# State-space weights taken in the transposed layout, first maxima without transposes between them, gathers that start before the weights are in

## The reference

```
h = emb[x]                                       # 2 x 2048 tokens, 256 wide
Q, K, V = heads(h @ w + b)                       # 16 heads of 16
o = softmax(Q K^T / 4) V ; h = o @ wo + bo
xn = layernorm(h)
for each direction (forward; backward on the flipped sequence):
    xh, z = split(xn @ in_w.T)                   # in_w 1024 x 256
    xc = silu(causal 4-tap convolution of xh)
    dt, Bm, Cm = split(xc @ xproj_w.T)           # xproj_w 48 x 512
    delta = softplus(dt @ dt_w.T + dt_b)         # dt_w 512 x 16
    state-space scan over the sequence; y = (scan + xc * D) * silu(z)
    add y @ out_w.T to h                         # out_w 256 x 512
h = h + low_rank_ffn(layernorm(h))
```

## Time and profile before

| | us |
|---|---|
| median of 3 runs | 3738.87 |
| lowest and highest | 3728.02, 3742.55 |
| the profiled execution's own time | 3733.11 |
| its span in the profile | 3731.3 |
| its mean granted TensorE clock | 0.946 |

### The profile page before, as it was taken

How to read it: one execution, slowest core, us unless ns; L and a number is a source line. 1 busy time by engine, 2 the same in 40 slices (tenths; PEclk the granted TensorE clock), 3 DMA queues, 4 the chain that set the end, 5 groups by cost and what they waited for, 6 DMA issues and landing times. The chain is left out here.

```text
span 3731.3 us, 70349 instructions
## 1 busy us (share of the span) xinstructions
PE 3335.9 (89%) x24001; PEld 1935.0 (52%) x24001; DVE 2932.7 (79%) x3002; ACT 2798.2 (75%) x4818; POOL 1536.1 (41%) x1252
## 2 busy tenths in 40 slices
PE   7699999999999999745999999999999999987798
PEld 4333333333333333232666767667766767665554
DVE  2579999899989999241899889988899899998122
ACT  2158888788878888713988888988889888986133
POOL 3000000000000000001888888888888898888000
PEclk9669999899989999977999999999999999999899
DMA  5530202022020200042111111211111111111422
GB/s 171 134 74 6 39 5 39 12 33 34 10 39 5 40 5 5 19 165 59 41 58 47 57 58 58 68 60 56 56 48 58 57 58 58 52 52 62 138 73 79
DMA packets 102538, 203.95 MB, mean 55 GB/s; under 512 B 19328, under 2 KB 36768, under 8 KB 100704
## 3 DMA queue, kind: packets, MB, share of 16 engines
q1 hardware_dynamic: 81616, 174.28, 16.5%
q10 hardware_dynamic: 19088, 21.37, 2.0%
q0 software_dynamic: 1536, 4.20, 0.5%
HBM read 144.23 MB, written 55.05 MB: 53 GB/s over the span
## 5 line engine op out<-in xcount | busy, mean ns | idle before, releaser
L1071 POOL TENSOR_TENSOR m_g<-m_hs,m_cb 128x512 f32<-128x512 f32 x1024 | 1296.3, 1290 | 215.5 <-DVE m_hs L1369 205.0
L657 DVE TENSOR_REDUCE a_mx<-a_ps_m 128x2 f32<-128x1024 f32 x1024 | 1244.2, 1224 | 122.0 <-PE a_ps_m L505 100.2
L627 ACT ACTIVATE a_probs<-a_ps_s 128x512 f32<-128x512 f32 x2048 | 1111.6, 596 | 201.8 <-PE a_ps_s L535 144.6
L1369 DVE TENSOR_TENSOR_SCAN m_hs<-m_da,m_carry,m_ps_x 128x512 f32<-128x512 f32 x768 | 956.8, 1270 | 104.5 <-PE m_ps_x L1144 64.0
L505 PE MATMUL a_ps_m<-a_k,a_q 48*128 48x512 f32 x2048 | 790.9, 469 | 31.7 <-DMA a_q<-q_scr 28.4
L535 PE MATMUL a_ps_s<-a_q,a_k 50*128 50x512 f32 x2048 | 773.5, 457 | 20.8 <-issue 10.7
L1144 PE MATMUL m_ps_x<-m_ident,m_bu 128*128 128x128 f32 x4096 | 637.8, 279 | 107.4 <-DVE m_hs L1369 95.3
L1287 ACT ACTIVATE m_da<-m_delta,m_a_cur 128x512 f32<-128x512 f32 x1024 | 720.7, 713 | 5.7 <-DVE m_hs L1369 5.6
L1144 PEld LDWEIGHTS m_ps_x<-m_ident,m_bu 128*128 128x128 f32 x4096 | 484.5, 143 | 448.9 <-issue 324.6
L542 PE MATMUL a_ps_o<-a_probs,a_v 128*32 128x256 f32 x8192 | 665.1, 397 | 8.7 <-ACT a_o L614 8.2
L1272 ACT ACTIVATE m_bu<-m_dut,m_bt 128x512 f32<-128x512 f32 x896 | 639.3, 714 | 27.3 <-PE m_ps_x L1144 27.1
(11 more groups left out here) (158 smaller groups left out, 2325.8 us busy)
## 6 DMA issues: line engine op xcount, KB each, us to landing
m_cb<-c_scr SPq DMA_DIRECT2D x128, 512.0 KB, 3.8
y_scr<-m_ysb SPq DMA_DIRECT2D x16, 1024.0 KB, 6.7
ffn_y<-y_scr SPq DMA_DIRECT2D x16, 1024.0 KB, 10.2
a_k<-k_scr SPq DMA_DIRECT2D x96, 128.0 KB, 7.5
a_q<-q_scr SPq DMA_DIRECT2D x96, 128.0 KB, 9.8
q_scr<-p_partsq SPq DMA_DIRECT2D x16, 512.0 KB, 3.3
k_scr<-p_partsk SPq DMA_DIRECT2D x16, 512.0 KB, 3.3
m_xn<-xn_scr SPq DMA_DIRECT2D x16, 512.0 KB, 4.9
```

Of the source, the lines that this page charges most:

```text
L627: nc.scalar.activation(probs[:, t % PR, HEADS[j]], turned(i), ACT.Exp, scale=float(DK) ** -0.5).then_inc(exped, 1)
L657: nc.vector.reduce_max(mx[:, i:i + wide], ps_m[:, b:b + wide], AX.X).then_inc(m_maxed, 1)
L1071: nc.gpsimd.tensor_tensor(g[:, t % NG], hs[:, t % NHS], cb[:, quarter % 2, n % CQ], ALU.mult).then_inc(g_ok, 1)
L1369: nc.vector.tensor_tensor_scan(hs[:, t % NHS, rev], da[:, t % NDA, rev], ps_x[:, t % NX, rev], carry[:, n, i:i + 1] if p else 0.0, ALU.mul ...
```

## The change

The four state-space weights of each direction are handed to the program already in the layout in which it uses them (`laid_out`, on the host, before the launch). `weight_transposes` and its scratch tensors are gone: eight loads, 64 transposes, their copies and eight stores. The later stages load the same bytes in the same shapes from the inputs. Of the four memsets of ones, the two for the second buffer go from DVE to POOL. In the embedding stage `rows_free` is raised before PE's waits for `ids_ok` and `w_in`; POOL still waits for `ids_ok` by itself.

```diff
@@ embed_and_project, PE
                 nc.tensor.transpose(ps_t[:, 0, 0:NI], ids_f[:, 3], ident[0:NI, 0:NI]).then_inc(ids_col, 1)
+                pe.sem_inc(rows_free, 2)
                 pe.wait_ge(ids_ok, ONE + 1)
                 pe.wait_ge(w_in, ONE + 96)
-                pe.sem_inc(rows_free, 2)
...
@@ attention
-        W_AFTER = BLK + HG * EARLY - w_count
-        W_NEG = w_count - HG * (EARLY - 2)
+        FIRST_NEG = BLK + 8
...
@@ attention, SyncE
                 load(0, 0, [0, 1], first_parts)
-                sp.wait_ge(ones_ok, ONE + 2)
+                sp.wait_ge(ones_first, ONE + 2)
                 load(0, 0, [0, 1], last_part)
                 load(0, 0, range(2, HG))
                 store_neg(0, 0, 0)
-                sp.wait_ge(ones_ok, ONE + 4)
+                sp.wait_ge(ones_ok, ONE + 2)
                 load(1, 1)
...
@@ attention, GpSimd
                 identity(nc.gpsimd, ident32[:, :], a_cleared, ident32_ok)
-                w_clear()
+                pool.wait_ge(ident32_ok, ONE + 1)
+                for i, first in enumerate((P // 4, 3 * P // 4)):
+                    nc.gpsimd.memset(k_st[first:first + P // 4, 1].bitcast(FP32), 1.0).then_inc(ones_ok, 1)
+                    pool.wait_ge(ones_ok, ONE + i + 1)
...
@@ attention, PE
-                max_blocks(0, 0, 0, 0, W_AFTER, loads)
-                for i in range(w_count):
-                    w_transpose(pe, i)
-                    if i == W_NEG:
+                for item in range(BLK + HG * EARLY):
+                    if item == FIRST_NEG:
                         transpose_neg(0)
-                    item = W_AFTER + i
                     max_blocks(item // BLK, 0, item // BLK, item % BLK, item % BLK + 1, loads if item < BLK else None)
-                pe.wait_ge(w_copied, ONE + w_count)
...
@@ attention, ACT
-                w_load(act)
-                for i in range(w_count):
-                    if i == W_NEG:
-                        copy_neg(0)
-                    w_copy(act, i)
-                w_store(act)
+                copy_neg(0)
...
-                act.wait_ge(w_stored, ONE + 8 * 16)
...
@@ attention, DVE
-                for buf in range(2):
-                    for first in (P // 4, 3 * P // 4):
-                        nc.vector.memset(k_st[first:first + P // 4, buf].bitcast(FP32), 1.0).then_inc(ones_ok, 1)
+                for first in (P // 4, 3 * P // 4):
+                    nc.vector.memset(k_st[first:first + P // 4, 0].bitcast(FP32), 1.0).then_inc(ones_first, 1)
...
@@ mamba, SyncE (and the like for xproj_w, dt_w and, in mamba_out_and_ffn, out_w)
-                    sp.dma_start(win[:, :, 0:DI], win_scr[z][:, 0:DI].rearrange("(k p) m -> p k m", p=P)).then_inc(win_x, 16)
+                    sp.dma_start(win[:, :, 0:DI], win_t[z][:, 0:DI].rearrange("(k p) m -> p k m", p=P)).then_inc(win_x, 16)
```

More of the change, by code:

```diff
@@ L305, in attention @@
-def attention(nc, sem, q_scr, k_scr, v_all, o_scr, weights):
+def attention(nc, sem, q_scr, k_scr, v_all, o_scr):
     with ExitStack() as ctx:
@@ L1018, in _ @@
                     sp.dma_start(a_cur[:, z], w["A_log"].rearrange("(k p) n -> p k n", p=P)).then_inc(w_in, 16)
[L1019 removed]
+                    sp.dma_start(wxp[:, z], xp_t[z]).then_inc(w_in, 16)
                     for first in (X_DT, X_DT2):
[L1021 removed]
+                        sp.dma_start(wdt[first:first + R, z], dtw_t[z]).then_inc(w_in, 16)
                 load_xn(1)
@@ L1383, in _, with mamba_out_and_ffn @@
                     gate(STEPS - 1, i)
-def mamba_out_and_ffn(nc, sem, y_scr, ow_scr, h_scr, u1, v1, b1, u2, v2, b2, out):
+def mamba_out_and_ffn(nc, sem, y_scr, ow_t, h_scr, u1, v1, b1, u2, v2, b2, out):
     NF = FF // P
@@ L1621, in lm_tower @@
     dirs = [{n: a[f"L0_attn_{z}_{n}"] for n in names} for z in "fb"]
+    win_t, xp_t, dtw_t, ow_t = ([w[n] for w in dirs] for n in ("in_w", "xproj_w", "dt_w", "out_w"))
     with nc.sbuf_tensor("v_all", [P, B, H // HG, NT, HG * DK], FP32) as v_all:
@@ L1627, in lm_tower @@
         with semaphores(nc) as sem:
-            attention(nc, sem, q_scr, k_scr, v_all, o_scr, (dirs, win_scr, xp_scr, dtw_scr, ow_scr))
+            attention(nc, sem, q_scr, k_scr, v_all, o_scr)
     with semaphores(nc) as sem:
@@ L1631, in lm_tower, with laid_out @@
     with semaphores(nc) as sem:
-        mamba(nc, sem, dirs, win_scr, xp_scr, dtw_scr, xn_scr, y_scr, c_scr)
+        mamba(nc, sem, dirs, win_t, xp_t, dtw_t, xn_scr, y_scr, c_scr)
     with semaphores(nc) as sem:
-        mamba_out_and_ffn(nc, sem, y_scr, ow_scr, h_scr, a["L0_ffn_U1"], a["L0_ffn_V1"], a["L0_ffn_b1"],
+        mamba_out_and_ffn(nc, sem, y_scr, ow_t, h_scr, a["L0_ffn_U1"], a["L0_ffn_V1"], a["L0_ffn_b1"],
                           a["L0_ffn_U2"], a["L0_ffn_V2"], a["L0_ffn_b2"],
                           out.rearrange("b (t p) d -> (b t) p d", p=P))
+def laid_out(name, value):
+    if name.endswith("_in_w") or name.endswith("_dt_w"):
+        return value.T
+    if name.endswith("_xproj_w"):
+        rows = np.zeros((XPW, DI), value.dtype)
+        for first, part in ((X_DT, slice(0, R)), (X_DT2, slice(0, R)), (X_B, slice(R, R + DS)), (X_C, slice(R + DS, R + 2 * DS))):
+            rows[first:first + part.stop - part.start] = value[part]
+        return rows.T.reshape(ND, P, XPW).transpose(1, 0, 2)
+    if name.endswith("_out_w"):
+        return value.T.reshape(ND, P, D).transpose(1, 0, 2)
+    return value
 def kernel(**inputs):
```

74 lines of the change are left out of this document (5 added, 69 removed).

## The result

| | before | after |
|---|---|---|
| median, us | 3733.44 (4 runs) | 3677.81 (4 runs) |
| lowest and highest, us | 3727.89, 3742.55 | 3664.22, 3690.49 |
| ratio, 95% interval | | 0.986 [0.983, 0.989] |
| the profiled execution's span, us | 3731.3 | 3662.4 |

The change is faster by 55.6 us in this comparison. So a fair figure for the gain is about 44 us, give or take 5, and the profiled execution after, the fastest of the 14, is not a typical one. What made it faster than the others is told with the jumps.

A forecast was written before the change was run, and what follows sets the result against it. Two early stretches were taken as on the path, 125 to 228 us held by PE's transposes at half clock. Terms 2.9 + 8.4 + 30.2 + 4.2 = 45.7 us off gave 3687.4 or 3693.2 by baseline; forecast 3690, range 3676 to 3704.

The forecast's parts named there:

- Gathers: Embedding stage: index copy no longer waits behind PE's weight wait, so PE's transposes start earlier; -2.9 us, between -1.5 and -3.1.
- First loads: Attention start: without weight loads on ACT's queue, first keys and queries land at 141.8, not 150.2; -8.4 us, -3 to -8.9.
- The later load that served as the measure: The same 24 DMAs alone, from 406.44 us: twelve are in 14.4 us after the first issue.
- First maxima: Maximum scores before the body: 42 pairs at 1.14 us without transposes, 47.8 instead of 78.0; -30.2 us, or -25.6 at 1.25.
- ACT: Body's start: no weight stores ahead of ACT's first exponential, so it follows the first score sooner; -4.2 us, -3.5 to -4.4.
- The clock: PE's half clock in the early body, 0.42 us lost per microsecond; left at 0, ends -5.3 and +6.
- The rest was to shift by 46 us: Sign of being right: everything after the first exponential shifted by 46 us, the body's 32 reduces in 40 us unchanged.
- Half clock far beyond the body's first 26 us: Sign of being wrong: half clock in the attention body lasting far beyond its first 26 us or so.
- Early clock: Rival: the clock rises during the first maxima, so the body starts at 2.4 GHz; 5.3 us more gained, 3685; chance 0.15.
- Small terms: Rival: loads at most 3 us earlier, reduces at 1.25, gathers worth 1.5; 11.4 us less gain, 3701; chance 0.19.
- Low clock in the body: Rival: half clock stays in the body; 109 us beyond the 12.6 eats the gain; slower, chance 0.02.
- Nothing in the maxima: Rival: something other than the transposes holds the first stretch; 3.9 + 4.2 + 8.4 = 16.5 us gained, near 3720; chance 0.03.

The follow-up runs named there:

- repeats: The changed kernel's own runs plus two experiments that turned out to be it over again; 14 runs, median 3686.4 us (3664.22 to 3697.06).
- stores_kept: Changed kernel with ACT's eight stores of the earlier sizes put back, writing the values' buffer to scratch nobody reads; 3686.59 us, ratio 0.989.
- after_sem127: Changed kernel with 127 increments of an unused semaphore in PE's list at the attention stage's start; 3699.43 us, ratio 0.991.
- transposes_kept: Changed kernel with 64 transposes of a constant put back between the maximum scores, and ACT's 64 copies, without loads or stores; 3721.84 us, ratio 0.997.

## Why the prediction was right

The forecast was 3690.0, and the changed kernel took 3677.81, within the range; over all repeats it is 3686.4. The mechanism was right in each of its four terms. That the first four runs lie 12 us under the forecast, near the low end of the range, is chance as far as the repeats can tell: they are closer to it.

**Gathers (2.9 booked).** The steps came as put: the copy at 5.74, PE at 14.88, no wait for the weights. At the attention stage's start about 2.5 is left, 1.5 in the first profile of after, between the value taken and the low bound. The bound's reason is seen in that profile: the granted clock rose at 24.0, as in before, so half of what was gained went into running at half clock for longer. (The same matmul of the projections takes 1.06 us ahead of this time and 0.59 behind it.) In the nine other profiles of the changed order it rose at 20.8 to 23.9, and more was kept. At an equal rise the term is 1.4: the stage's start less half the time of the rise is 112.9 to 113.1 in the three profiles of the kernel before, and 111.4 to 111.8 in the eleven with the early gathers. The rest of the 2.5 is the clock's.

**First loads (8.4 booked).** 7.3 by the profiles with and without the weight loads. The later load that served as the measure was right: 14.8 us from the first issue to PE's pairs (140.45 - 125.64), for the 14.4 said. Oversized was the other side: before's own profile had its loads some 1 us later than the other three profiles that had them (25.14 against 23.74 to 24.38). A term taken from one execution carries that execution's chance.

**First maxima (30.2 booked).** 29.7. The maxima took 48.3 for the 47.8 said, a pair of scores each 1.13, with PE waiting for DVE 0.34 us in each. Turning the maxima stayed hidden.

**ACT (4.2 booked).** 4.3. The reason said, that ACT issued stores as the body began, holds with the addition of `stores_kept`: it was their place behind the last copy.

**The clock (0 booked, -5.3 to +6).** This was the mis-sized part of the argument. The prediction looked at the half clock of the body's start alone: it ended 8.5 to 30.1 us behind the first exponential in the 14 profiles (12.6 in before), so even there the bound of +6, for 14 us more, was short: 17.5 us more came, which is 7.4. Its price of 0.42 for each microsecond was right: without a pause, the time from the first exponential to the next chunk's small stores is 37.9 us with 12.5 us of half clock in it, 41.8 with 21.4 and 45.5 with 30.1, in both kernels on one line. And the term was not nothing: the four profiles of the kernel before have 12.5 to 23.3 us of half clock there, mean 16.3, the nine of the changed order without transposes 15.0 to 32.4, mean 25.0, which gives some 4 us of the gain back. The larger part, the two jumps back, was seen in the earlier trace rows and used as a warning only. It stands for 8 to 38 us in a run and moves mostly by chance. The change also took one pause out of each jump, which the prediction did not have; the profiles put it at some 10 us, with over 4 of error, and the times at less. So the 43.8 of the four terms and the 44 of the times agree in part because these two went opposite ways. The jumps move what four runs show, and they are the larger part of why the first comparison gave 55.6 for a change of about 44.

**Signs that it had named.** The rest was to shift by 46 us: it did by 43.7 at the first exponential, and by 56.8 and 68.9 further on in the first profile. Half clock far beyond the body's first 26 us was to be a sign of being wrong: it ended 31 us behind the first transposed score at the latest, but came back in `after` until 239. A changed time in the later stages was to be something unseen: the 12.1 us there are within what the profiles differ by.

**The sums.** They come out, but for one: in the rival in which something other than the transposes holds the first stretch, the 3.9 of 3.9 + 4.2 + 8.4 stands in no row; with the gathers' 2.9 it would be 15.5, and 3721 for 3720. Nothing rests on it.

**The rivals.** Early clock: refuted. From 140 to 188 us PE did only matmuls, two each 1.13 us, but for the one transpose at 181.50, at 0.50 throughout:

```profile
140.00:188.00 48.00, 33.04 (x84) 12.21 (x84) 46.17 (x42) 0.42 (x2) 1.42 (x2) 0.50 0.24 28
```

The Trainium skill, "TensorE: Matmul & The Clock Gate", Part 4, says that transposes do not count as PE activity in the same way; no run here shows that they are what kept this stretch at half clock, since it stays there without the 64. Small terms: the gathers and the loads were each smaller than booked, together by 1.5, far from the 11.4 of that case. Low clock in the body: half clock ended within 31 us of the body's start in all 14 profiles, and all half clock in the body together came to 90 us at most (in `after_sem127`), where this rival needs 109 beyond the 12.6. Nothing in the maxima: refuted by `transposes_kept`.

## What to carry to other kernels

Work put into a stretch because an engine "has time there" costs in full once it makes that engine the slower one: 64 transposes of under half a microsecond took PE from waiting for DVE to being waited for, and cost 30 us. Read a stage's intervals from its own first mark, over several profiles, before a term is believed; the total of one execution here moved by 28 us with no edit at all. Where a loop on the critical engine jumps back only a few times, writing it out is worth a try; then look for the next engine that jumps.

## What the hardware showed that was not expected

- A jump back of PE's loop stopped PE for 2.7 to 3.4 us, and depending on the loop's place in the list (moved by about 128 instructions) a second time for 1.7 to 2.6. Writing the loop out removed both. A packet of 16 KB on the queue read as PE's for instructions begins 2.4 to 3.6 us before the end of each of these pauses. The Trainium skill, "Runtime: NRT & Kernel Launch", "Instruction fetch mechanics", says that a taken branch whose target is not in the small window held on chip waits for its fetch, which these runs agree with; it gives no duration for it.
- Behind a pause of about 3 us PE spent between 3.4 and 47.8 us at half clock, with the same dense work, and the length differed between executions of one program. Even a wait of 1.1 to 1.2 us was followed by 13.7 and 27.3 us of it, and twice by none. What sets the length stays open.
- Eight stores of ACT, under way beside four small ones of SyncE, took the time from the first small one to SyncE's next load from 4.19 to 8.06 us, with the DMA engines full at 384 GB/s.
- Beside 24 loads of 128 KB such a packet of PE's instructions took 1.60 to 1.86 us instead of about 1, and began late, up to 260 records of PE later than without them; in the two latest of six cases PE stopped for 2.3 and 2.6 us.
